# Border of the last stage of a two-layer gated transformer: two norms and three copies on VectorE, another order, three banks each for maxima and scores

## Chip, cores and metric

One core of a Trainium2 chip runs the kernel. The metric is the device time in microseconds of one execution, inputs and outputs in HBM. Engines: PE (TensorE matmul), VectorE (DVE in the rows), ACT (ScalarE), POOL (GpSimd), SP (SyncE, which here only issues DMAs).

## The reference

Sixteen batches of 256 tokens of width 256, all float32, through four gated residual steps. Only the last two matter here.

```python
x = x + jnp.tanh(g_xattn[0]) * _L0_xattn_ref(_layernorm(x, axis=-1), ctx_1024, ctx_1024)   # decayed running sum
x = x + jnp.tanh(g_ffn[0]) * _L0_ffn_ref(_layernorm(x, axis=-1), w_gate, w_up, w_down)     # fp4-quantised
x = x + jnp.tanh(g_xattn[1]) * _L1_xattn_ref(_layernorm(x, axis=-1), ctx_1024, ctx_1024, 16)
x = x + jnp.tanh(g_ffn[1]) * _L1_ffn_ref(_layernorm(x, axis=-1), w_fc, b_fc, w_proj, b_proj)
```

The third is attention with 16 heads of width 16, rotary embedding, a bias by position and a softmax. The fourth is `gelu(q(x) @ q(w_fc).T + b_fc)`, quantised again by `q`, times `q(w_proj).T`. `q` rounds blocks of 32 values to 3 bits behind the exponent of the block's largest magnitude.

## The kernel before, in words

The program is written engine by engine; the order on each engine is the order in its function, and semaphores (`wait_ge`, `then_inc`) tie them. `over_batches` calls a body once for each batch. A `Batch` has `shifted(n)`, the batch n further on or None past either end. `first`, `last` and `lead[0]` to `lead[5]` are batches 0, 15 and 0 to 5.

All of x stays in SBUF (`xres`). The first layer runs until about 337 us, attention from there to about 662, and the last stage, the second feed-forward, to the end. The eight PSUM banks of attention are two each: `a_ps_t` (for turned inputs), `a_ps_m` (products for the row maxima), `a_ps_s` (scores), `a_ps_pv` (values).

**Attention** (`at_body`). While batch b is exponentiated, b+1 is turned and its row maxima are taken, and b+2 is prepared. PE turns queries and keys in eight steps (`at_turn`, L586) that ACT copies out (`at_turned`, L953). Then come 16 groups m0 to m15 of products for the maxima (`at_scores_for_max`, L606), each of which VectorE reduces (`at_row_max`, L1558), with scores s2 to s15 between them (`at_scores`, L627; s0 and s1 stand in the turning). ACT exponentiates each score group (`at_exponent`, L962). After every two, PE multiplies with the values (`at_times_v`, L642, groups 0 to 7, quads of two), and ACT copies a quad out (`at_pv_out`, L968). PE turns this back (`at_turn_out`, L650) and VectorE adds it to `xres` (`at_add_attention`, L1565 to L1572), called the residual here. Even and odd groups use different halves of the array's rows.

Before the change m0 to m3, m6, m7, m10, m11, m14 and m15 lie in the two `a_ps_m` banks and the others in the two `a_ps_t` banks, so that from m6 on a group waits for the maximum four groups back; m2 and m3 wait for the one two back, m4 and m5 for none. A score waits for the exponential two back.

**The border.** The last attention batch has no next batch to turn. Into its place come: w3 and w4, the weights of the last stage, which GpSimd has rounded to codes and which PE turns (`turn_w34`) and ACT copies out (`w34_out`, L832); and the inputs of the leading batches. An input is made in these steps: statistics on VectorE (`ff_input_stats`), the power -1/2 on GpSimd (`ff_input_rstd`, L1228), the shift on VectorE (`ff_input_shift`), the norm on ACT (`ff_norm`, L1011), on VectorE the block's power of two, called its magic (`ff_input_magic`, L1622 to L1629), on GpSimd the sum with it (`ff_input_up`, L1234), on VectorE the codes (`ff_input_codes`, L1635), on PE the turning (`ff_turn_input`, L703) and on ACT the copy (`ff_input_out`, L1018).

**The last stage** (`ff_body`). PE makes four groups of 512 hidden values (`ff_fc`, L716 and L718), ACT the gelus (`ff_gelu`, L1024), VectorE their magic (`ff_hidden_magic`, L1643 to L1650), GpSimd the sum (`ff_hidden_up`, L1241), VectorE the codes (`ff_hidden_codes`, L1659), PE turns them (`ff_turn_hidden`) and multiplies with w4 (`ff_proj`, L743), and VectorE adds the residual (`ff_add_ffn`). In the body of batch b VectorE does hidden magic b+1, statistics b+6, codes b+3, hidden codes b and input magic b+4. `ff_hidden_magic(lead[0])` stands ahead of the loop.

The order of VectorE at the border before, from L1743 on:

```python
ff_input_stats(lead[0]); ff_input_stats(lead[1]); ff_input_shift(lead[0]); ff_input_shift(lead[1])
ff_input_magic(lead[0]); ff_input_stats(lead[2]); ff_input_shift(lead[2]); ff_input_codes(lead[0])
ff_input_magic(lead[1]); ff_input_stats(lead[3]); ff_input_codes(lead[1]); ff_input_shift(lead[3])
at_add_attention(last)
ff_input_magic(lead[2]); ff_input_stats(lead[4]); ff_input_codes(lead[2]); ff_input_shift(lead[4])
ff_input_magic(lead[3]); ff_input_stats(lead[5]); ff_hidden_magic(lead[0])
```

## Time and profile before

| | us |
|---|---|
| median of 3 runs | 815.8 (814.9 to 817.67) |
| the profiled execution | 816.15 |
| its span, first to last instruction | 814.0 |
| PE busy (matmul) | 701.7, 86% |
| VectorE busy | 691.9, 85% |
| ACT busy | 486.2, 60% |
| GpSimd busy | 431.4, 53% |
| mean granted clock of TensorE | 0.941 of 2.4 GHz |

Times in the rows are counted from the first instruction. Busy time of PE includes the tail of each pipelined matmul. What stands in brackets at the end of a timeline row is the idle time of the engine before it and what ended it. Neighbouring instructions of one line are merged, and "x2" tells how many. The largest groups of instructions are the exponentials (256 of 602 ns on ACT), the maxima (256 of 686 ns on VectorE) and the scores (512 matmuls on PE).

### The profile page before, as it was taken

How to read it: one execution, taken by the hardware profiler on the slowest of the kernel's cores; microseconds unless marked ns; L12 is line 12 of the kernel's file. 1: busy time of each engine (PE TensorE's matmuls, PEld its weight loads, DVE VectorE, ACT ScalarE, POOL GpSimd, SP SyncE). 2: the span in 40 equal slices, each digit the busy share in tenths (PEclk: the TensorE clock that was granted, in tenths of full speed). 3: DMA queues.
4: the chain of work that ended last, by engine and by line, in shares of the span. 5: the costliest groups of instructions: out<-in, count | busy, mean ns of one | idle time of the engine just before them, and what ended most of it. 6: DMA issues, size and time to landing. Idle time of an engine off the chain costs nothing.

```text
span 814.0 us, 16554 instructions
## 1 busy us (share of the span) xinstructions
PE 701.7 (86%) x5075; PEld 516.7 (63%) x5090; DVE 691.9 (85%) x1230; ACT 486.2 (60%) x955; POOL 431.4 (53%) x331
## 2 busy tenths in 40 slices
PE   1476999999999998789999999999999876877685
PEld 1365888888888876556666666666666433544454
DVE  5996888888888878779999999989898649999995
ACT  3354555455454443348887787888788674566653
POOL 3634664656656555644445555554444526665553
PEclk9588999999999999889999999999999687999998
DMA  8800000000000000010000000000001000100011
GB/s 271 252 33 0 2 1 1 0 0 0 0 0 1 1 2 0 1 53 2 3 3 1 1 1 2 1 1 1 1 1 53 2 1 0 40 26 26 27 39 52
DMA packets 17719, 18.35 MB, mean 23 GB/s; under 512 B 1670, under 2 KB 16912, under 8 KB 17680
## 3 DMA queue, kind: packets, MB, share of 16 engines
q1 hardware_dynamic: 17084, 17.66, 6.6%
q8 instruction: 21, 0.34, 0.2%
q10 hardware_dynamic: 596, 0.20, 0.1%
q14 instruction: 18, 0.15, 0.1%
HBM read 13.39 MB, written 4.19 MB: 22 GB/s over the span
## 4 chain that ended last, share of the span: by engine, by line
PE 56%; DVE 22%; issue 9%; ACT 6%; POOL 3%; DMA 1%; DVEq 1%; POOLq 0%; ACTq 0%
PE ps_o L547 9%; PE a_ps_t L586 7%; PE a_ps_pv L642 7%; PE a_ps_s L627 5%; PE a_ps_m L606 5%; DVE f_ps_small L1643 4%; PE ps_gu L511 4%; PE ps_gu L513 4%; PE ps_gu L512 4%; DVE f_hcode L1659 4%; PE a_ps_t L606 3%; DVE maxima L1558 2%; PE a_ps_pv L650 2%; ACT stack_t L953 1%; ACT probs L962 1%
## 5 line engine op out<-in xcount | busy, mean ns | idle before, releaser
L962 ACT ACTIVATE probs<-a_ps_s 128x512 f32<-128x512 f32 x256 | 147.8, 602 | 29.9 <-PE a_ps_s L627 25.4
L1558 DVE TENSOR_REDUCE maxima<-a_ps_m 128x2 f32<-128x512 f32 x160 | 103.0, 686 | 11.5 <-PE a_ps_m L606 11.3
L627 PE MATMUL a_ps_s<-stack_t 64*128 64x256 f32 x512 | 101.9, 314 | 3.4 <-ACT probs L962 1.8
L1192 POOL TENSOR_TENSOR stack<-roped,stack 128x512 f32<-128x512 f32 x32 | 42.7, 1335 | 109.7 <-DVE stack L1548 108.3
L547 PE MATMUL ps_o<-w2t,hqt 128*128 128x256 f32 (+1 forms) x384 | 99.1, 392 | 1.3 <-ACT hqt L880 0.7
L511 PE MATMUL ps_gu<-w1h,yth 128*128 128x352 f32 x256 | 87.5, 342 | 9.1 <-DVE h L1364 5.9
L953 ACT CAST stack_t<-a_ps_t 128x512 fp32r<-128x512 f32 x128 | 71.8, 585 | 31.5 <-PE a_ps_t L586 31.5
L642 PE MATMUL a_ps_pv<-probs,v_aug 128*32 128x256 f32 x1024 | 84.9, 404 | 2.9 <-ACT probs L962 2.9
L586 PE MATMUL a_ps_t<-idf,stack 128*128 128x128 f32 x512 | 77.2, 292 | 8.8 <-POOL stack L1192 5.1
L512 PE MATMUL ps_gu<-w1l,yth 128*128 128x352 f32 x256 | 84.1, 328 | 0.0
L513 PE MATMUL ps_gu<-w1h,ytl 128*128 128x352 f32 x256 | 83.8, 327 | 0.0
L547 PEld LDWEIGHTS ps_o<-w2t,hqt 128*128 128x128 f32 (+1 forms) x384 | 66.3, 189 | 22.1 <-issue 12.4
L627 PEld LDWEIGHTS a_ps_s<-stack_t 64*128 64x128 f32 x512 | 67.7, 190 | 16.7 <-ACT probs L962 9.4
L586 PEld LDWEIGHTS a_ps_t<-idf,stack 128*128 128x128 f32 x512 | 58.3, 147 | 25.4 <-ACT stack_t L953 8.4
L1558 DVE TENSOR_REDUCE maxima<-a_ps_t 128x2 f32<-128x512 f32 x96 | 63.1, 686 | 10.9 <-PE a_ps_t L606 10.9
L1159 POOL TENSOR_TENSOR hq<-hcode,hscale 128x1408 f32<-128x1408 bf16 x16 | 41.5, 2591 | 56.5 <-DVE hcode L1383 56.5
L606 PE MATMUL a_ps_m<-stack_t 64*128 64x256 f32 x320 | 66.3, 323 | 3.7 <-DVE maxima L1558 2.7
L872 ACT ACTIVATE sg<-ps_gu 128x352 f32<-128x352 f32 x64 | 29.7, 464 | 66.3 <-PE ps_gu L513 66.3
L606 PEld LDWEIGHTS a_ps_m<-stack_t 64*128 64x128 f32 x320 | 43.3, 188 | 34.3 <-DVE maxima L1558 18.8
L1241 POOL TENSOR_TENSOR f_hup<-f_h,f_hmag 128x2048 f32<-128x2048 f32 x16 | 58.2, 3640 | 9.1 <-DVE f_hcode L1659 8.1
L1024 ACT ACTIVATE f_h<-f_ps_fc 128x512 f32<-128x512 f32 x64 | 34.9, 596 | 42.0 <-POOL f_hup L1241 39.2
L511 PEld LDWEIGHTS ps_gu<-w1h,yth 128*128 128x128 f32 x256 | 49.4, 193 | 12.3 <-DVE h L1364 7.3
(181 smaller groups left out, 1680.9 us busy)
## 6 DMA issues: line engine op xcount, KB each, us to landing
xres<-in_x SPq DMA_DIRECT2D x16, 256.0 KB, 3.2
ctx<-in_ctx SPq DMA_DIRECT2D x16, 256.0 KB, 3.8
out_x<-f_y SPq DMA_DIRECT2D x16, 256.0 KB, 2.1
w1a_raw<-in_w_gate_up SPq DMA_DIRECT2D x1, 1024.0 KB, 7.3
w_raw<-in_w_fc SPq DMA_DIRECT2D x1, 1024.0 KB, 5.7
w_raw<-in_w_proj SPq DMA_DIRECT2D x1, 1024.0 KB, 4.8
w_raw<-in_w_down SPq DMA_DIRECT2D x1, 704.0 KB, 9.7
stack_t<-neg_max_t SPq DMA_DIRECT2D x32, 8.0 KB
```

What stands on the lines that cost most here:

```text
L511: nc.tensor.matmul(into, yth[:, kc, c, :], w1h[:, kc, cols], start=kc == 0, stop=False)
L512: nc.tensor.matmul(into, yth[:, kc, c, :], w1l[:, kc, cols], start=False, stop=False)
L513: ins = nc.tensor.matmul(into, ytl[:, kc, c, :], w1h[:, kc, cols], start=False, stop=kc == KD - 1)
L547: ins = nc.tensor.matmul(ps_o[:, c, :], hqt[0:rows, g, n, :], w2t[0:rows, k, :], start=k == 0, stop=k == KH0 - 1)
L586: ins = nc.tensor.transpose(a_ps_t[:, g % 2, (n * C + c) * P:(n * C + c + 1) * P], a_stack[:, b.par, which, c, 2 * pair:2 * pair + 2, :].r ...
L606: ins = nc.tensor.matmul(max_bank(m)[:, n, :], a_stack_t[b.par][rows, 0, pair, c * P:(c + 1) * P], a_stack_t[b.par][rows, 1, pair, :], sta ...
L627: ins = nc.tensor.matmul(a_ps_s[:, half, n, :], a_stack_t[b.par][rows, 1, pair, kc * P:(kc + 1) * P], a_stack_t[b.par][rows, 0, pair, :], ...
L642: ins = nc.tensor.matmul(a_ps_pv[32 * n:32 * n + 32, quad % 2, 0:T], a_v_aug[:, b.par, kc, 4 * quad + n, :], a_probs[:, (2 * g + n % 2) % ...
L953: nc.scalar.copy(a_stack_t[b.par][:, g % 2, pair:pair + 2, :].rearrange("p a t -> p (a t)"), a_ps_t[:, g % 2, :]).then_inc(a_t, 1)
L962: nc.scalar.activation(a_probs[:, u % 8], a_ps_s[:, u % 2], ACT.Exp).then_inc(a_exp, 1)
L1241: nc.gpsimd.tensor_tensor(f_blocks(f_hup[:, :]), f_blocks(f_h[:, b.par]), f_spread(f_hmag[:, b.par], F_NBH), ALU.add).then_inc(f_g_hup, 1)
L1558: nc.vector.tensor_reduce(a_maxima[:, b.par, c, 4 * quad + half:4 * quad + half + 3:2], max_bank(m), X, ALU.max).then_inc(a_v_max, 1)
```

## The change

- Three banks each: m_k lies in `a_ps_t[0]` if k mod 3 is 1, in `a_ps_m[0]` if it is 2, else in `a_ps_m[1]`. From s4 on a score lies in `a_ps_t[1]` or one of the `a_ps_s` banks by the same rule, in every batch but the last.
- `w34_out` is split: ACT copies w3 (`w3_out`), VectorE copies w4 (`w4_out`), earlier, since PE turns w4 after m=4 and no longer after m=8. PE turns the first input after m=10, not m=12.
- The norms of leading batches 2 and 3 go from ACT to VectorE, also named `ff_norm`.
- The copy of the last quad of values goes from ACT to VectorE (`at_last_pv_out`).
- VectorE's residual of the last batch goes behind the inputs of batches 2 and 3 and the statistics of 4 and 5; GpSimd's steps are reordered.

```diff
         def max_bank(m):
-            pair, half = m // 2, m % 2
-            if pair >= 2 and pair % 2 == 0:
-                return a_ps_t[:, half, :].rearrange("p (a t) -> p a t", t=T)
-            return a_ps_m[:, half]
+            if m % 3 == 1:
+                return a_ps_t[:, 0, :].rearrange("p (a t) -> p a t", t=T)
+            return a_ps_m[:, 0 if m % 3 == 2 else 1]
+        def score_bank(b, u):
+            if u < 4 or not b.shifted(1):
+                return a_ps_s[:, u % 2]
+            if u % 3 == 1:
+                return a_ps_t[:, 1, :].rearrange("p (a t) -> p a t", t=T)
+            return a_ps_s[:, 0 if u % 3 == 2 else 1]
+        def last_in_score_bank(b, u):
+            if not b.shifted(1):
+                return u - 2
+            return {2: 0, 3: 1, 5: 2, 6: 3}.get(u, u - 3)
+        M_LAST_IN_T, U_LAST_IN_T = MU - 3, SU - 3
...
 # at_turn
-                elif b.shifted(-1):
-                    pe.wait_ge(a_v_max, b.shifted(-1).count(MU, 2 * LAST_IN_TURN_BANKS + g + 1))
+                elif b.shifted(-1) and g == 0:
+                    pe.wait_ge(a_v_max, b.shifted(-1).count(MU, M_LAST_IN_T + 1))
+                elif b.shifted(-2):
+                    pe.wait_ge(a_exp, b.shifted(-2).count(SU, U_LAST_IN_T + 1))
 # at_scores_for_max
-                if m == 0 and b.shifted(-1):
+                if m >= 3:
+                    pe.wait_ge(a_v_max, b.count(MU, m - 2))
+                elif m == 1:
+                    pe.wait_ge(a_t, b.count(TG, TG - 1))
+                elif m == 2 and b.shifted(-1):
                     pe.wait_ge(a_mt, b.shifted(-1).count(1, 1))
-                if m in (4, 5):
-                    pe.wait_ge(a_t, b.count(TG, TG + m - 5))
-                elif m >= 2:
-                    pe.wait_ge(a_v_max, b.count(MU, group_in_same_max_bank(m) + 1))
                 elif b.shifted(-1):
-                    pe.wait_ge(a_v_max, b.shifted(-1).count(MU, MU + m - 1))
+                    pe.wait_ge(a_v_max, b.shifted(-1).count(MU, MU))
 # at_scores
-                if u >= 2:
-                    pe.wait_ge(a_exp, b.count(SU, u - 1))
+                if u == 4 and b.shifted(1):
+                    pe.wait_ge(a_t, b.shifted(1).count(TG, TG))
+                elif u >= 2:
+                    pe.wait_ge(a_exp, b.count(SU, last_in_score_bank(b, u) + 1))
 # at_body of PE
-                    if not nxt and m == 8:
+                    if not nxt and m == 4:
                         turn_w34(2)
                         turn_w34(3)
-                    if not nxt and m == 12:
+                    if not nxt and m == 10:
                         ff_turn_input(lead[0])
                 if not nxt:
-                    pe.wait_ge(a_w34, 4)
+                    pe.wait_ge(v_w4, 2)
 # at_body of ACT
-                    if not nxt and u == 9:
-                        w34_out(2)
-                        w34_out(3)
-                    if not nxt and u in (3, 7, 11):
+                    if not nxt and u in (3, 7):
                         ff_norm(lead[u // 4])
-                    if not nxt and u == 14:
+                    if not nxt and u == 12:
                         ff_input_out(lead[0])
-                at_pv_out(b, 3)
+                if nxt:
+                    at_pv_out(b, 3)
 # ACT, ahead of the last stage's loop
             ff_input_out(lead[1])
-            ff_norm(lead[3])
 # GpSimd, ahead of the last stage's loop
-            for b in lead[:3]:
-                ff_input_rstd(b)
+            ff_input_rstd(lead[0])
+            ff_input_rstd(lead[1])
             ff_input_up(lead[0])
+            ff_input_rstd(lead[2])
+            ff_input_up(lead[1])
             ff_input_rstd(lead[3])
-            ff_input_up(lead[1])
+            ff_input_up(lead[2])
             ff_input_rstd(lead[4])
-            ff_input_up(lead[2])
             ff_input_rstd(lead[5])
 # VectorE
+            def w4_out(at):
+                dve.wait_ge(t_w34, at + 3)
+                nc.vector.tensor_copy(w_proj_t[:, 4 * at:4 * at + 4, :].rearrange("p k n -> p (k n)"),
+                                      a_ps_m[:, at].rearrange("p a t -> p (a t)").bitcast(BF16)).then_inc(v_w4, 1)
+            def at_last_pv_out(b):
+                dve.wait_ge(a_t_pv, b.count(PG, PG))
+                dve.wait_ge(a_t_out, b.shifted(-1).count(2, 2))
+                nc.vector.tensor_copy(a_pv_t[:, 3, :], a_ps_pv[:, 1, 0:T]).then_inc(a_pv, 1)
+            def ff_norm(b):
+                dve.wait_ge(f_v_shift, b.count(1, 1))
+                dve.wait_ge(f_g_up, b.shifted(-2).count(1, 1))
+                for c in range(C):
+                    nc.vector.tensor_scalar(f_xn[:, b.par, c * D:(c + 1) * D], tiles(xres, b)[:, c, :], f_rstd[:, b.par, c:c + 1],
+                                            f_shift[:, b.par, c:c + 1], ALU.mult, ALU.add).then_inc(f_a_norm, 1)
...
             ff_input_magic(lead[0])
+            w4_out(0)
+            w4_out(1)
             ff_input_stats(lead[2])
             ff_input_shift(lead[2])
             ff_input_codes(lead[0])
             ff_input_magic(lead[1])
+            ff_norm(lead[2])
             ff_input_stats(lead[3])
             ff_input_codes(lead[1])
+            ff_input_magic(lead[2])
             ff_input_shift(lead[3])
-            at_add_attention(last)
-            ff_input_magic(lead[2])
+            ff_norm(lead[3])
             ff_input_stats(lead[4])
             ff_input_codes(lead[2])
+            ff_input_magic(lead[3])
             ff_input_shift(lead[4])
-            ff_input_magic(lead[3])
+            at_last_pv_out(last)
             ff_input_stats(lead[5])
+            at_add_attention(last)
             ff_hidden_magic(lead[0])
```

## Rows read from the trace of the kernel before

**Rows 1.** Windows: us, busy us (instructions) of each engine, granted clock, DMA share, GB/s.
```profile
...
374.00:621.00 247.00, 239.25 (x2265) 160.62 (x2262) 225.09 (x438) 198.72 (x402) 120.89 (x90) 1.00 0.01 3
645.65:654.25 8.60, 8.34 (x64) 4.44 (x62) 4.85 (x18) 7.40 (x15) 3.44 (x4) 0.60 0.00 0
663.34:670.71 7.37, 4.14 (x18) 1.74 (x20) 4.88 (x20) 5.98 (x12) 1.72 (x2) 0.93 0.00 1
...
661.00:666.00 5.00, 3.75 (x24) 2.06 (x23) 3.93 (x13) 4.94 (x9) 0.02 (x1) 1.00 0.00 0
672.00:814.00 142.00, 100.97 (x746) 65.48 (x757) 125.29 (x206) 78.24 (x123) 81.73 (x39) 0.90 0.09 30
```

**Rows 2.** Waits from 356 to 616: who for whom, total us, times, longest.
```profile
...
DVE maxima L1558 <- PE a_ps_t L606: 7.2, 14, 0.6
```

**Rows 3.** Timeline of VectorE, one batch: start, us, operation [idle before].
```profile
...
604.11 2.58 DVE L1558 TENSOR_REDUCE maxima<-a_ps_m 128x2 f32<-128x512 f32 x4 [0.47 <-PE a_ps_m L606]
607.23 1.29 DVE L1558 TENSOR_REDUCE maxima<-a_ps_t 128x2 f32<-128x512 f32 x2 [0.54 <-PE a_ps_t L606]
...
610.83 0.69 DVE L1548 CAST stack<-roped 128x1024 fp32r<-128x1024 f32 x1
...
614.42 1.29 DVE L1558 TENSOR_REDUCE maxima<-a_ps_m 128x2 f32<-128x512 f32 x2
```

**Rows 4.** Timeline of PE, the same batch.
```profile
...
604.17 0.64 PE L642 MATMUL a_ps_pv<-probs,v_aug 128*32 128x256 f32 x8
604.86 0.50 PE L606 MATMUL a_ps_m<-stack_t 64*128 64x256 f32 x2
...
606.12 0.64 PE L642 MATMUL a_ps_pv<-probs,v_aug 128*32 128x256 f32 x8
606.69 0.51 PE L606 MATMUL a_ps_t<-stack_t 64*128 64x256 f32 x4
...
612.30 0.64 PE L642 MATMUL a_ps_pv<-probs,v_aug 128*32 128x256 f32 x8
...
614.86 0.64 PE L642 MATMUL a_ps_pv<-probs,v_aug 128*32 128x256 f32 x8 [0.24 <-ACT probs L962]
```

**Rows 5.** Timeline of ACT, the same batch.
```profile
...
613.45 0.60 ACT L962 ACTIVATE probs<-a_ps_s 128x512 f32<-128x512 f32 x1 [0.42 <-PE a_ps_s L627]
...
614.20 0.61 ACT L962 ACTIVATE probs<-a_ps_s 128x512 f32<-128x512 f32 x1
```

**Rows 6.** Timeline of VectorE, the border.
```profile
...
661.33 0.26 DVE L1565 RECIPROCAL denom<-a_ps_pv 128x16 f32<-128x16 f32 x1 [7.08 <-PE a_ps_pv L650]
...
670.71 2.28 DVE L1643 TENSOR_REDUCE f_ps_small<-f_h 128x64 f32<-128x2048 f32 x1
...
673.55 2.29 DVE L1643 TENSOR_REDUCE f_ps_small<-f_h 128x64 f32<-128x2048 f32 x1
```

**Rows 7.** Timeline of PE, the border.
```profile
...
649.09 1.89 PE L463 MATMUL a_ps_m<-idb,w_codes 128*128 128x128 bf16 x16
...
660.64 1.09 PE L650 MATMUL a_ps_pv<-idf,pv_t 128*128 128x128 f32 x8 [0.49 <-ACT pv_t L968]
...
662.86 0.39 PE L703 MATMUL f_ps_h<-idb,f_xcode 128*128 128x128 bf16 x4
664.50 0.39 PE L716 MATMUL f_ps_fc<-bias,ones 128*128 128x512 bf16 x1 [1.25 <-ACT f_xt L1018]
```

**Rows 8.** Timeline of ACT, the border.
```profile
...
656.62 0.63 ACT L962 ACTIVATE probs<-a_ps_s 128x512 f32<-128x512 f32 x1
...
661.90 2.06 ACT L1024 ACTIVATE f_h<-f_ps_fc 128x512 f32<-128x512 f32 x4
...
665.35 2.54 ACT L1024 ACTIVATE f_h<-f_ps_fc 128x512 f32<-128x512 f32 x4
```

**Rows 9.** Two lines of VectorE: count, ns min/median/max, first and last start.
```profile
...
L1527 DVE TENSOR_SCALAR qn<-xres,a_mv,a_rstd x26: 400/822/1252, 378.2 to 601.3; 128x256 f32 x24, 128x256 f32<-128x256 f32 x2
...
L1659 DVE TENSOR_TENSOR f_hcode<-f_hup,f_hmag x32: 1211/1218/1227, 678.1 to 805.2; 128x1024 bf16<-128x1024 f32 x32
```

More of the change, by code:

```diff
@@ L626, in at_scores @@
                     pair = 2 * quad + n
-                    ins = nc.tensor.matmul(a_ps_s[:, half, n, :], a_stack_t[b.par][rows, 1, pair, kc * P:(kc + 1) * P],
+                    ins = nc.tensor.matmul(score_bank(b, u)[:, n, :], a_stack_t[b.par][rows, 1, pair, kc * P:(kc + 1) * P],
                                            a_stack_t[b.par][rows, 0, pair, :], start=True, stop=True)
@@ L961, in at_exponent @@
                     act.wait_ge(a_t_pv, b.shifted(-1).count(PG, (u + 8) // 2 + 1))
-                nc.scalar.activation(a_probs[:, u % 8], a_ps_s[:, u % 2], ACT.Exp).then_inc(a_exp, 1)
+                nc.scalar.activation(a_probs[:, u % 8], score_bank(b, u), ACT.Exp).then_inc(a_exp, 1)
             def at_pv_out(b, quad):
```

20 lines of the change are left out of this document (8 added, 12 removed).

## The prediction

> **What bounds the kernel now.** I read the windows by stage first, then the waits and the timelines of one attention batch and of the border. In the attention loop PE is busy 239 of 247 us and VectorE 225, at the full granted clock of 2.4 GHz (1.00); in the last stage VectorE is busy 125 of 142 us and PE 101 [rows 1]. So the loop is a close race of two engines, and the last stage is VectorE's: what moves VectorE's start there moves the end.
>
> The loop takes sixteen batches, 18.4 and 18.6 us in turn. Each has a stretch of turning and one of sixteen max groups m0 to m15, between which PE does scores s2 to s15 and seven value groups. VectorE reduces a group every 0.60 us and has one hole: after m3 it is idle 0.54 us until m4 arrives [rows 3]. The waits show it in 14 batches of 14, 7.2 us in all [rows 2]. Its reason stands on PE: m2 and m3 wait for the maxima of m0 and m1 (one bank apart), each breaks PE's stream, the second value group starts only at 606.12 and m4 at 606.69 [rows 4]. The stretch is closed by another chain: s14 and s15, their exponentials at 613.45 and 614.20 with a copy of values between, and the last value group at 614.86, after which the next turn starts at 615.43 [rows 4, 5].
>
> At the border VectorE waits from 654.25 to 661.33 for the last attention's turned output: the residual stands ahead of the inputs of batches 2 to 4. It takes all these up behind it and reaches the first hidden magic at 670.71, though the gelus it needs had ended at 663.96; the second starts at 673.55 [rows 6, 8]. From there on VectorE hardly rests.
>
> **The change, part one: three banks each.** m_k now waits for the maximum of m_(k-3), and the scores rotate through three banks. I walk the batch from 603.49 with the durations of [rows 3 to 5], a wait's latency 0.05. m2 has nothing to wait for and starts when value group 0 ends (604.17 + 0.57 = 604.74 against 604.86); m3 waits only for m0's maximum (604.81) and goes beside it. Value group 1 then starts at 605.53 (606.12 before) and m4 at 606.10 (606.69): 0.59 earlier. The data are there at 606.60, VectorE comes free at 606.55, so its hole shrinks from 0.54 to about 0.05. From then VectorE is fed without a break and is 0.59 early.
> PE meets new waits, because the max groups had four banks in the second half and have three: value group 3 ends at 609.0, m9 waits for m6's maximum until 609.18 (0.19); m10 for m7's until 609.79 (0.25); m12 for m9's. m9's maximum follows the cast at 610.83 by 0.60 and ends now at 610.83 + 0.60 + 0.69 - 0.59 = 611.53, so m12 and s13 start at 611.6 after 0.44 idle, and value group 5 at 612.02 instead of 612.30. Behind it s14 is ready 0.31 earlier, the exponentials move from 613.45 to 613.14 and the last value group from 614.86 to 614.55. So of the 0.59 gained in front, 0.31 reach the next turn. The turn of a batch waits for m13's maximum and an exponential of the batch before; both are over 1 us old. The last max group's reduction ends 0.1 us after that turn starts, as the turning of the maxima comes 0.9 us later it hides.
> The loop has 14 such batches besides the one with w4's magic, in which VectorE is the bound and a hole of 0.5 us is traded for a PE block one group earlier (0), and the first one, where PE runs at the lower clock and the turn waits one maximum longer (0.0, bounds -0.3 and +0.4). Sum: 14 x -0.31 = -4.3 us. Bounds: -0.59 x 14 = -8.3 (all of it arrives) and 0.
>
> **Part two: the border, ahead of the residual.** VectorE's new list: magic 0 (ends 645.73 as before), two w4 copies, everything it had between, two norms; then the copy of the last values, stats 5, the residual, hidden magic 0.
> *w4 copies.* PE turns w4 right after s6, by the order of its instructions at about 645.5 (an estimate: four score groups, 0.43 us each at the low clock, and a value group less than now) instead of 649.09; the 16 transposes take 1.9 us at this stretch's clock of 0.60 [rows 1, 7]. The second bank is there at 647.4. VectorE's copy of 1024 columns isn't in the trace; nearest are 1.22 us (1024 elements of codes, two inputs) [rows 9] and 0.69 (the cast of 1024) [rows 3]. I take 1.1, so 648.5; with the ends 648.1 to 648.7. PE's and ACT's work doesn't grow: ACT loses two copies of 1.0 and a norm, which shortens its way to its last exponential by some 1.3 us (656.6 to 657.2 before [rows 8]).
> *Norms.* The same form on 128x256 takes 0.40 us in its shortest case, 0.82 as median, 1.25 at most [rows 9]. The long ones overlap GpSimd's elementwise work. Here each norm starts in the moment in which a magic also releases GpSimd's up step, so I take about 1.5 for each pair, 3.0 for both; bounds 1.5 and 5.0. The Trainium skill's page "SBUF — State Buffer" (section "SBUF: two separate sides") says that a VectorE operation in a two-port mode and a GpSimd operation hold one shared port pair exclusively, whichever starts first; by it both pairs of norms lose one up step each, by a free port the forecast would be 1.5 us lower. The 1.25 against 0.40 agrees with the lock.
> *The list's length.* The work from 645.65 to the wait was 4.85 us busy and that behind the residual up to the first hidden magic 4.88 [rows 1]; less 1.2 for stats 5, which stay behind, 8.5 us. With norms 3.0 and one exposed wait for GpSimd's power step of batch 2 (0.85: its start used to be covered, now nothing of VectorE stands between): 648.5 + 8.5 + 3.0 + 0.85 = 660.9. Call it D. The last value group is out by 659, so VectorE is later than PE there: the 7.08 us of idle is filled and the last values' copy starts at D.
> *Behind D.* What is queued on PE behind that copy: the turned output, which waits for it, the last two groups of batch 0's first product (2.22 us from 660.64 to 662.86 [rows 7]), then batch 1's. With 0.45 for the copy the gelus of batch 0 end at D + 3.4 = 664.3; before near 664.0. ACT's table load, which stood between the last value copy and the first of these gelus, now goes under the wait. Batch 1's four products and gelus took 664.50 to 667.89, 3.4 us [rows 7, 8]; with ACT's input copy ahead they end at D + 7.2 = 668.1. VectorE: copy 0.4, stats 5 1.2, residual 2.0 (661.33 to 663.34 before, where the window begins [rows 1, 6]), first hidden magic at D + 3.8 = 664.7 instead of 670.71, over at 667.5; the second starts at 668.2 instead of 673.55. After it stand the same steps as before, with GpSimd's hidden up released 6 us earlier, and VectorE full. **Gain 5.3 us**, bounds below.
>
> **Sum.** The profiled execution is 816.15 us (span 814.0), 0.35 above the median of 815.8. 816.15 - 4.3 - 5.3 = **806.6 us**.
>
> **Rivals.**
> *The border at the lower clock.* PE's clock is 1.00 from 661 to 666 but 0.60 from 645 to 654 [rows 1]. The change leaves PE with some 2 us of nothing before D. If the products behind it then run at 1.2 GHz, they take twice as long: 1.7 more to the gelus of batch 0, 2.5 more for batch 1, so the second hidden magic comes at 672.4, and the border gives 1.1 only: 816.15 - 4.3 - 1.1 = 810.7. For it: the idle is new. Against: PE was idle there before, and had the full clock right after. "TensorE: Matmul & The Clock Gate" of the Trainium skill (section "HAM oscillation — how this bites in real kernels") says that a gap in PE's work sends it to half rate, and the next burst pays; by it this rival is the case.
> *The loop gives nothing.* The new waits ahead of m9, m10 and m12 sum to 0.9 us of PE and eat the 0.59: 816.15 - 5.3 = 810.9. For: PE has only 8 us of idle in 247.
> *The loop gives the whole hole:* 816.15 - 8.3 - 5.3 = 802.6. For: VectorE and PE are both early; against: the chain over the exponentials closes the stretch.
> *Slower: the three-bank ring.* PE takes its instructions in order; a max group that waits holds the scores and the value group behind it, and these feed ACT. If the front isn't won (m4 still late, because s4 now waits for the last turned copy, or m3 doesn't run beside m2), the 0.9 us of waits stay with some 0.5 exposed in each batch: 14 x 0.5 = +7.0, and 816.15 + 7.0 - 5.3 = 817.9 (822 with the lower clock). It decides from +0.38 us a batch, where it eats the border's 5.3.
> *The change doesn't do what it says:* VectorE's list is much longer (norms at 5.0, copies at 1.22, more waits for GpSimd), D beyond 666: 816 with an idle loop.
>
> **How the numbers follow.** Forecast 0.45, lower clock 0.15, loop nothing 0.17, whole hole 0.12, no gain at all 0.05, slower 0.06. The range 802.5 to 813.0 holds the first four and the mixtures of the second and third. A run can be told from no change beyond 0.3%, here 2.4 us: faster 0.86, same 0.07, slower 0.07.
>
> **What would show it.** Right: batches of 18.1 and 18.3 us; the idle of VectorE ahead of m4 below 0.1 (now 0.54); waits of PE for maxima ahead of the second half's groups; the last value group 0.3 nearer to the start of the stretch. At the border VectorE idle under 2 us between 641 and 665 of before's time, the second hidden magic 27.2 us behind the end of the last residual but one, at 641.0 (32.5 now). Wrong: a period above 18.5, a granted clock under 0.8 over batch 1's products, norms over 1.25 each, or a VectorE that reaches the value copy before PE's last value group ends.

## The result, and the profile after

The changed kernel takes 810.02 us (median of 6 runs, 809.08 to 810.57) against 815.74 (6 runs, 813.4 to 817.86) for the kernel before: ratio 0.9919, 95% interval 0.9905 to 0.9934. Faster, as forecast, and inside the range; but 3.4 us above the 806.6 forecast. The profiled execution took 810.57, its span is 808.5 (814.0 before).

A period is the time from one turning of the maxima on PE to the next; sixteen batches make fifteen of them. Stage by stage, the 5.5 us of span are: up to the first reduction of maxima +1.1 (340.08 to 341.17; code that the change doesn't touch), 14 periods of the loop (the first and 13 ordinary ones) -3.28, the last period 0.0 (20.15 and 20.14), from the last turning of the maxima to the second hidden magic -2.11, from there to the last hidden magic 0.0 (121.50 and 121.54), and the rest -1.30 (19.00 to 17.70). Two of the six terms are the change's: 5.4 us, where 9.6 were forecast.

Windows of the changed kernel (us, busy us (instructions) of PE, PEld, VectorE, ACT, POOL, granted clock, DMA share, GB/s), which answer to [rows 1]:
```profile
374.00:618.80 244.80, 231.62 (x2277) 148.86 (x2278) 224.84 (x439) 200.71 (x403) 121.61 (x91) 1.00 0.01 3
...
656.00:661.00 5.00, 0.77 (x10) 0.29 (x4) 4.77 (x15) 1.05 (x2) 1.92 (x2) 0.93 0.01 2
661.00:663.50 2.50, 2.50 (x11) 1.85 (x11) 1.80 (x8) 0.00 (x0) 1.57 (x2) 0.50 0.00 0
663.50:666.00 2.50, 1.56 (x11) 0.66 (x9) 1.60 (x3) 1.67 (x3) 0.14 (x1) 0.95 0.00 0
```
The first row is the loop. Between 661 and 663.5 PE works without a pause at clock 0.50, 1.2 GHz. Before, 661 to 666 had 1.00 [rows 1].

**The loop.** VectorE (start, us, operation [idle before <- what ended it]) in the batch that answers to [rows 3]. Lines are shifted by the edit: maxima L1579, maximum products L619, values L657.
```profile
602.21 0.69 DVE L1579 TENSOR_REDUCE maxima<-a_ps_m 128x2 f32<-128x512 f32 x1 [0.82 <-PE a_ps_t L619]
602.82 0.68 DVE L1579 TENSOR_REDUCE maxima<-a_ps_t 128x2 f32<-128x512 f32 x1
603.42 1.28 DVE L1579 TENSOR_REDUCE maxima<-a_ps_m 128x2 f32<-128x512 f32 x2
604.73 0.69 DVE L1579 TENSOR_REDUCE maxima<-a_ps_t 128x2 f32<-128x512 f32 x1
```
The hole before m4 is gone: from 602.21 to the end of the stretch there is no idle entry. But the idle ahead of the first maximum is 0.82 instead of 0.47 [rows 3]. What VectorE won in the middle it spends waiting for the next batch, since another chain sets that. The waits tell the same: the row of [rows 2] is now this one, and it means another place. A reader who only looks at the total would think that the wait ahead of m4 grew from 7.2 us.
```profile
DVE maxima L1579 <- PE a_ps_t L619: 11.4, 14, 0.9
```
PE in that batch, for [rows 4]:
```profile
601.59 0.38 PE L619 MATMUL a_ps_m<-stack_t 64*128 64x256 f32 x1
...
604.19 0.38 PE L619 MATMUL a_ps_t<-stack_t 64*128 64x256 f32 x1
...
609.67 0.38 PE L619 MATMUL a_ps_m<-stack_t 64*128 64x256 f32 x1 [0.29 <-DVE maxima L1579]
...
610.11 0.64 PE L657 MATMUL a_ps_pv<-probs,v_aug 128*32 128x256 f32 x8
...
612.67 0.64 PE L657 MATMUL a_ps_pv<-probs,v_aug 128*32 128x256 f32 x8 [0.26 <-ACT probs L975]
```
m4 starts 2.60 us behind m0, before 3.20 (603.49 to 606.69); value group 5 at 8.52, forecast 8.53; the last value group at 11.08, before 11.37: 0.3 earlier, as walked.

**The border.** VectorE, for [rows 6]:
```profile
646.15 1.47 DVE L1512 COPY w_proj_t<-a_ps_m 128x1024 bf16<-128x1024 bf16 x2 [1.72 <-PE a_ps_m L474]
...
649.63 0.16 DVE L1636 SCALAR_TENSOR_TENSOR f_shift<-f_ps_small,f_rstd 128x2 f32<-128x2 f32 x1 [0.82 <-POOL f_rstd L1238]
...
651.33 1.46 DVE L1643 TENSOR_SCALAR f_xn<-xres,f_rstd,f_shift 128x256 f32<-128x256 f32 x2
...
660.23 0.42 DVE L1518 COPY pv_t<-a_ps_pv 128x256 f32<-128x256 f32 x1
...
665.23 2.29 DVE L1671 TENSOR_REDUCE f_ps_small<-f_h 128x64 f32<-128x2048 f32 x1 [0.87 <-ACT f_h L1035]
...
669.24 2.29 DVE L1671 TENSOR_REDUCE f_ps_small<-f_h 128x64 f32<-128x2048 f32 x1 [1.12 <-ACT f_h L1035]
```
The 7.08 us of idle are filled, the two waits at the end are new: VectorE stands before both hidden magics until their gelus end. PE, for [rows 7]:
```profile
639.21 0.51 PE L642 MATMUL a_ps_s<-stack_t 64*128 64x256 f32 x4 [2.10 <-DMA stack_t<-neg_max_t]
...
655.85 0.64 PE L657 MATMUL a_ps_pv<-probs,v_aug 128*32 128x256 f32 x8
660.71 1.97 PE L665 MATMUL a_ps_pv<-idf,pv_t 128*128 128x128 f32 x8 [4.23 <-DVE pv_t L1518]
...
662.90 1.02 PE L733 MATMUL f_ps_fc<-w_fc_t,f_xt 128*128 128x512 bf16 x2
...
663.97 0.59 PE L733 MATMUL f_ps_fc<-w_fc_t,f_xt 128*128 128x512 bf16 x2
```
PE waits 4.23 us for the value copy, then the turned output takes 1.97 us (1.09 before) and a pair of products 1.02, a moment later 0.59. And ACT, for [rows 8]: the load of the gelu's table indeed lies ahead of the wait, but two of batch 0's gelus wait 6.91 us for the products queued behind the turned output.
```profile
654.67 1.28 ACT L1035 ACT_TABLE_LOAD   x1
655.96 1.08 ACT L1035 ACTIVATE f_h<-f_ps_fc 128x512 f32<-128x512 f32 x2
663.96 1.25 ACT L1035 ACTIVATE f_h<-f_ps_fc 128x512 f32<-128x512 f32 x2 [6.91 <-PE f_ps_fc L733]
```

### The profile page after: what moved, and what is told of

Read it like the earlier page. It is cut to its first block, busy times and chain, and to the rows that moved or that the text cites. A ratio compares the mean times of both kernels' runs of the same rounds, so it can differ in the third digit from the quotient of the medians.

```text
span 808.5 us, 16554 instructions
## 1 busy us (share of the span) xinstructions
PE 691.2 (85%) x5075; PEld 503.9 (62%) x5090; DVE 694.7 (86%) x1237; ACT 483.2 (60%) x948; POOL 432.8 (54%) x331
## 4 chain that ended last, share of the span: by engine, by line
PE 50%; DVE 26%; issue 11%; ACT 5%; DMA 3%; POOL 2%; DVEq 1%; SPq 1%; POOLq 0%; ACTq 0%
PE ps_o L558 9%; PE a_ps_t L599 7%; DVE maxima L1579 5%; PE a_ps_pv L657 5%; PE ps_gu L522 4%; PE ps_gu L524 4%; PE ps_gu L523 4%; DVE f_hcode L1687 4%; DVE f_ps_small L1671 4%; PE a_ps_s L642 3%; PE a_ps_m L619 3%; DMA ctx<-in_ctx 2%; PE a_ps_t L619 2%; PE a_ps_pv L665 2%; ACT stack_t L966 1%
## 5 line engine op out<-in xcount | busy, mean ns | idle before, releaser
L1579 DVE TENSOR_REDUCE maxima<-a_ps_m 128x2 f32<-128x512 f32 x176 | 116.1, 681 | 16.8 <-PE a_ps_t L619 11.3
L975 ACT ACTIVATE probs<-a_ps_s 128x512 f32<-128x512 f32 x196 | 115.7, 601 | 24.3 <-PE a_ps_s L642 19.6
L619 PE MATMUL a_ps_m<-stack_t 64*128 64x256 f32 x352 | 80.9, 327 | 10.2 <-DVE maxima L1579 8.8
L657 PE MATMUL a_ps_pv<-probs,v_aug 128*32 128x256 f32 x1024 | 83.6, 399 | 3.5 <-ACT probs L975 3.5
L642 PE MATMUL a_ps_s<-stack_t 64*128 64x256 f32 x392 | 79.3, 312 | 4.5 <-DMA stack_t<-neg_max_t 2.1
L619 PEld LDWEIGHTS a_ps_m<-stack_t 64*128 64x128 f32 x352 | 50.1, 187 | 50.9 <-issue 29.3
L642 PEld LDWEIGHTS a_ps_s<-stack_t 64*128 64x128 f32 x392 | 53.7, 189 | 14.7 <-issue 6.6
L1579 DVE TENSOR_REDUCE maxima<-a_ps_t 128x2 f32<-128x512 f32 x80 | 54.5, 681 | 3.2 <-PE a_ps_t L619 2.6
```

Source lines behind the costliest of these rows:

```text
L619: ins = nc.tensor.matmul(max_bank(m)[:, n, :], a_stack_t[b.par][rows, 0, pair, c * P:(c + 1) * P], a_stack_t[b.par][rows, 1, pair, :], sta ...
L642: ins = nc.tensor.matmul(score_bank(b, u)[:, n, :], a_stack_t[b.par][rows, 1, pair, kc * P:(kc + 1) * P], a_stack_t[b.par][rows, 0, pair, ...
L657: ins = nc.tensor.matmul(a_ps_pv[32 * n:32 * n + 32, quad % 2, 0:T], a_v_aug[:, b.par, kc, 4 * quad + n, :], a_probs[:, (2 * g + n % 2) % ...
L975: nc.scalar.activation(a_probs[:, u % 8], score_bank(b, u), ACT.Exp).then_inc(a_exp, 1)
L1579: nc.vector.tensor_reduce(a_maxima[:, b.par, c, 4 * quad + half:4 * quad + half + 3:2], max_bank(m), X, ALU.max).then_inc(a_v_max, 1)
```

## The experiments

The columns are read from the timelines of each kernel's profiled execution. "Loop" is the time over 14 periods, from the first turning of the maxima to the last but one. The next five columns count from the last turning of the maxima (636.51 before, 634.31 in the changed kernel): first score of the last batch, which waits for the DMA of its row maxima; last value copy; first and second hidden magic; and the second less what the first score lies beyond 3.47, which differs by up to 1.4 between runs with the same code there. "Ratio" is to the kernel before on the same chip.

| kernel | ratio, interval | loop | score | value copy | magic 0 | magic 1 | less score |
|---|---|---|---|---|---|---|---|
| before | 1 | 260.01 | 3.47 | 23.70 | 34.19 | 37.04 | 37.04 |
| changed | 0.9919, 0.9905 to 0.9934 | 256.73 | 4.90 | 25.92 | 30.92 | 34.93 | 33.50 |
| after_again (changed) | 0.9914, 0.9896 to 0.9932 | 256.59 | 4.03 | 25.14 | 30.36 | 34.36 | 33.80 |
| banks_only | 0.9968, 0.9952 to 0.9984 | 256.76 | 3.71 | 23.45 | 33.94 | 36.79 | 36.55 |
| border_only | 0.9959, 0.9944 to 0.9973 | 261.11 | 3.47 | 24.55 | 29.42 | 33.42 | 33.42 |
| max3_score2 | 0.9969, 0.9956 to 0.9982 | 261.34 | 4.17 | 25.85 | 29.72 | 33.39 | 32.69 |
| max2_score3 | 1.0169, 1.014 to 1.0197 | 274.02 | 3.47 | 24.54 | 29.76 | 33.76 | 33.76 |
| residual_first | 0.9947, 0.9929 to 0.9966 | 256.64 | 4.43 | 21.93 | 32.00 | 34.85 | 33.89 |
| warm_pe | 0.992, 0.9891 to 0.995 | 256.67 | 3.47 | 25.13 | 31.99 | 35.99 | 35.99 |
| products_ahead | 0.9901, 0.9877 to 0.9926 | 256.64 | 3.48 | 24.55 | 29.13 | 31.98 | 31.97 |
| magic_ahead | 0.9912, 0.9896 to 0.9928 | 256.67 | 3.47 | 24.56 | 26.09 | 33.16 | 33.16 |
| norms_on_act | 0.9903, 0.9886 to 0.9919 | 256.79 | 3.69 | 24.03 | 30.55 | 33.40 | 33.18 |
| w4_on_act | 0.9883, 0.9866 to 0.99 | 256.67 | 4.10 | 24.69 | 29.78 | 32.62 | 31.99 |
| ahead_and_norms | 0.9895, 0.988 to 0.991 | 256.67 | 4.23 | 25.91 | 27.95 | 35.03 | 34.28 |

The landing moves the value copy with it: with the same amount taken off, the copy starts 24.49 behind the turning in the changed kernel, 24.58 in after_again and 24.55 in border_only.

Stages that no kernel here edits also differ: the first reduction starts between 338.7 and 341.9, the tail behind the last hidden magic is 17.7 or 18.7 to 19.4, and from the second hidden magic to the last it takes 121.0 to 121.6, but 122.29 in max2_score3 and 123.17 in banks_only. So the ratios tell parts of 2 us and more, and the columns tell smaller ones. But the columns stand for one execution, and not always a typical one: that of residual_first is the fastest of 12 (808.09, median 811.9), those of w4_on_act and ahead_and_norms are the slowest of 5 (810.25 and 810.36, medians 808.16 and 808.35).

**banks_only** and **border_only**: one part each. The first keeps before's orders, norms and copies and has the three-bank rings, the second the reverse. The changed kernel ran beside them as **after_again**, unedited.
```diff
 # border_only, on the changed kernel
-            if m % 3 == 1:
-                return a_ps_t[:, 0, :].rearrange("p (a t) -> p a t", t=T)
-            return a_ps_m[:, 0 if m % 3 == 2 else 1]
+            pair, half = m // 2, m % 2
+            if pair >= 2 and pair % 2 == 0:
+                return a_ps_t[:, half, :].rearrange("p (a t) -> p a t", t=T)
+            return a_ps_m[:, half]
...
```


> The kernel before with nothing but the new banks and their waits. Theory A, the two parts of the change add up and the loop's is the larger: attention periods of 18.14 and 18.31 us (18.36 and 18.62 before), from first value group to first max group 11.08 and 11.16 us (11.38 and 11.47), and a time 3.4 us below the kernel before. Theory B, the loop's gain is only real together with a border that takes it up, because VectorE at the border waits for PE: the periods fall the same, but under 1.5 us of it reach the end. Forecast of the prediction for this part alone: -4.3 us.

> The changed kernel with the banks and waits of before in the attention loop. Theory A: periods 18.36 and 18.62 as before, and a time 2.1 to 3.6 us below the kernel before: 5.3 as forecast, less 1.8 for PE's low clock behind the last value copy, less up to 1.4 for a late landing of the last batch's row maxima. Theory B (the gains belong together): 4 us or more.

> The changed kernel once more, unchanged, for a second profile. In the first one PE began the last batch's scores 4.90 us after the turning of the maxima, 3.47 before the change; and the last value copy was followed by products at 1.2 GHz. Theory C, chance: 3.5 us this time, and a border (from the last turning of maxima to the second hidden magic) of 33.5 in place of 34.9 us. Theory D, a cost of the change (what PE, SyncE and ACT do there is not moved, so I doubt it): 4.9 again. The clock: low again behind the value copy, as PE is idle for over 4 us ahead of it whatever the phase.

Measured: 813.67, 812.74 and 809.23 us against 816.28. The rings alone give periods of 18.14 and 18.30 and a border of 36.8, the border alone 18.37 and 18.6 and a border of 33.4. By ratio the parts are -2.6 and -3.3 us, and the whole change is -7.0 beside them: they add, within the intervals, and both are real. The border's 3.6 us in the trace (37.04 to 33.42) are what the edit is worth when the DMA of the row maxima lands as it did before. In border_only's loop column two things hide that the edit doesn't touch: its first period is 20.84 (19.71 before), and its last, which the column leaves out, 19.23 (20.15 before), with the clock at 1.00 over its last 4 us where before it was 0.57. max3_score2's last period is short in the same way, 19.04.

after_again has PE's idle time and lower clock behind the value copy once more:
```profile
659.77 1.73 PE L665 MATMUL a_ps_pv<-idf,pv_t 128*128 128x128 f32 x8 [2.42 <-DVE pv_t L1518]
...
661.73 1.06 PE L733 MATMUL f_ps_fc<-w_fc_t,f_xt 128*128 128x512 bf16 x2
```
The idle is 2.42 us here, for 4.23 in the first trace, and the lower level is the same.

**max3_score2** and **max2_score3**: only one of the two rings has three banks.
```diff
 # max3_score2
-            if u < 4 or not b.shifted(1):
-                return a_ps_s[:, u % 2]
-            if u % 3 == 1:
-                return a_ps_t[:, 1, :].rearrange("p (a t) -> p a t", t=T)
-            return a_ps_s[:, 0 if u % 3 == 2 else 1]
+            return a_ps_s[:, u % 2]
...
 # max2_score3
-            if m % 3 == 1:
-                return a_ps_t[:, 0, :].rearrange("p (a t) -> p a t", t=T)
-            return a_ps_m[:, 0 if m % 3 == 2 else 1]
+            return a_ps_m[:, m % 2]
...
```


> The changed kernel with three banks for the maxima but the two of before for the scores, each score waiting for the exponential two back. Theory E, the maxima's ring gives nearly all: periods within 0.06 us of 18.14 and 18.31, time within 0.8 us of the changed kernel. Theory F, the third score bank is what lets PE run ahead to m4 (s6 and s7 no longer wait for the exponentials two back): periods 0.15 us or more longer, time 2 to 3.5 us above the changed kernel, and VectorE's hole ahead of m4 back to 0.3 us or more.

> The changed kernel with only the two a_ps_m banks for the maxima, each group waiting for the maximum two back, and three banks for the scores. The ring of three for the maxima alone (scores on two) had given nothing: periods 18.45 and 18.68. Theory F1, the scores' third bank alone makes the loop's gain: periods near 18.14 and 18.31. Theory F2, both are needed, since a maxima ring of two stops PE ahead of each group until VectorE is through, and VectorE then has a hole ahead of every group of a value pair: periods 18.6 or more, time 4 us or more above the changed kernel.

Measured: periods of 18.45 and 18.68 without the third score bank, a little longer than before's, and 19.44 and 19.58 without the third maximum bank. VectorE's waits, max3_score2:
```profile
DVE maxima L1571 <- PE a_ps_t L613: 11.4, 14, 0.9
DVE maxima L1571 <- PE a_ps_m L613: 8.8, 16, 2.9
```
and max2_score3:
```profile
DVE maxima L1575 <- PE a_ps_m L615: 26.4, 42, 2.9
```
In the changed kernel the wait for `a_ps_m` is 3.7 us in 2 times; in max3_score2 it comes 14 more times, once in a batch, and is 5.1 us more. That PE's scores wait for an exponential again and hold the maximum groups behind them is my reading of PE's order, and not shown by itself. The gain of 0.2 to 0.3 us a batch needs both rings; neither gives it alone, and each alone is a loss against the kernel before, whose maxima had four banks in the second half of a batch.

max3_score2 shows one thing more, at the border. Its last values come late, PE is idle only 0.55 us ahead of the turned output, and the order behind the value copy is that of the changed kernel:
```profile
661.71 1.09 PE L657 MATMUL a_ps_pv<-idf,pv_t 128*128 128x128 f32 x8 [0.55 <-DVE pv_t L1510]
...
662.85 0.59 PE L725 MATMUL f_ps_fc<-w_fc_t,f_xt 128*128 128x512 bf16 x2
```
At the full clock it is 7.54 us from the value copy to the second hidden magic, where the changed kernel took 9.01.

**residual_first**: the last value copy and the residual at the place where the kernel before had the residual; norms and w4 copies as in the changed kernel.
```diff
             ff_input_codes(lead[1])
+            at_last_pv_out(last)
+            at_add_attention(last)
             ff_input_magic(lead[2])
...
-            at_last_pv_out(last)
             ff_input_stats(lead[5])
-            at_add_attention(last)
             ff_hidden_magic(lead[0])
```


> The changed kernel with the last value copy and the last batch's residual ahead of the third input magic, near their old place; all else as changed. Theory G, the order is what fills VectorE's idle time: VectorE waits about 2 us for PE's last value group and 1.5 for the turned output, the first hidden magic comes about 33.3 us behind the last turning of maxima (30.4 and 30.9 changed), the second 36.1 (34.4 and 34.9), the time 1.3 to 2 us above the changed kernel. Theory H, the order hardly matters, since PE then has no long idle and keeps its clock, and batch 1's products come early: the second hidden magic within 0.5 us of the changed kernel's.

VectorE:
```profile
653.72 0.42 DVE L1518 COPY pv_t<-a_ps_pv 128x256 f32<-128x256 f32 x1 [2.05 <-PE a_ps_pv L657]
654.90 0.26 DVE L1586 RECIPROCAL denom<-a_ps_pv 128x16 f32<-128x16 f32 x1 [0.75 <-PE a_ps_pv L665]
...
663.79 2.28 DVE L1671 TENSOR_REDUCE f_ps_small<-f_h 128x64 f32<-128x2048 f32 x1
...
666.64 2.29 DVE L1671 TENSOR_REDUCE f_ps_small<-f_h 128x64 f32<-128x2048 f32 x1
```
VectorE idles 2.8 us before and in the residual, but the gelus are long done when it comes to the hidden magics, which stand back to back. The second comes at 33.89 (less score) against 33.50 and 33.80, within 0.5 us as the second theory said. So in this trace the order of which the change consists at this place is worth 0.1 to 0.4 us: it turns 2.8 us of idle ahead of the residual into 2.0 us ahead of the hidden magics. The other 3.2 us of the border (37.04 to 33.89) come with the other moves, the copies, the norms and the earlier turnings, taken together; no run parts them.

The medians don't settle it. By ratio residual_first is 2.3 to 2.7 us slower than the changed kernel, more than the first theory's 1.3 to 2, and the intervals hardly overlap. Its twelve executions spread from 808.09 to 814.99, and the trace is of the fastest. What the order is worth in a typical execution stays open.

**warm_pe**: 16 more matmuls on PE between the last value group and the turned output, whose result nobody reads.
```diff
+            for _ in range(16):
+                nc.tensor.matmul(f_ps_h0[:, :], idb[:, :], w_fc_t[:, 0, 0:512], start=True, stop=True)
             at_turn_out(last)
```


> The changed kernel with 16 matmuls whose results nobody reads (128x128 by 512 columns, into the bank of the first input's turned codes) between the last value group and the turned output, where PE is idle for 4.2 us. Theory I, PE's low clock behind the value copy costs the border 1.5 us: the turned output takes 0.9 us (1.97 changed), the gelus of batch 0 end 3.5 us after the value copy starts (5.0 and 5.2), the second hidden magic comes 1.5 us earlier, time 1.5 us lower. Theory J, the low clock is hidden by VectorE's own residual, or the clock falls whatever PE does: no change.

PE:
```profile
657.47 4.15 PE L813 MATMUL f_ps_h<-w_fc_t,idb 128*128 128x512 bf16 x16
661.46 1.04 PE L665 MATMUL a_ps_pv<-idf,pv_t 128*128 128x128 f32 x8
...
662.55 0.59 PE L733 MATMUL f_ps_fc<-w_fc_t,f_xt 128*128 128x512 bf16 x2
```
The filler was too long: the value copy came at 657.60, the turned output had to wait until 661.46, and magic 1 is 2.2 to 2.5 us later than in the changed kernel. Some 0.6 of that is not the filler's: the value copy itself waited 0.51 for PE's last values, which came at the lower clock. So neither theory held. But the price of the clock can be read: with PE at 1.00 the turned output is 1.04 instead of 1.97, and from its start to the last gelu of batch 0 it is 3.0 us instead of 4.5. The lower clock costs 1.5 us there.

**products_ahead**: the products that need no attention output go ahead of the turned output, so that PE has them to do while it would wait.
```diff
-            at_turn_out(last)
...
-            for u in range(4):
-                ff_fc(lead[1], u)
+            ff_fc(lead[1], 0)
+            ff_fc(lead[1], 1)
+            at_turn_out(last)
+            ff_fc(lead[1], 2)
+            ff_fc(lead[1], 3)
```


> The changed kernel with PE's second half of batch 0's products, batch 1's turned input and the first two of batch 1's products moved ahead of the turned output, into PE's idle 4.2 us. They need nothing from VectorE's value copy; in the order of the changed kernel they are queued behind it. Theory K, what is queued on PE behind the copy sets the second hidden magic: VectorE doesn't wait for gelus any more (0.87 and 1.12 us of idle ahead of the two magics), the first comes 30.0, the second 32.9 us behind the last turning of maxima (30.4 and 34.4 changed), time 1.5 to 2 us below the changed kernel. Theory L, the last stage is paced by GpSimd's hidden sum or ACT and gives it back within two batches: the second magic is early, the time the same.

VectorE:
```profile
658.67 0.42 DVE L1520 COPY pv_t<-a_ps_pv 128x256 f32<-128x256 f32 x1
...
661.25 0.26 DVE L1588 RECIPROCAL denom<-a_ps_pv 128x16 f32<-128x16 f32 x1 [0.96 <-PE a_ps_pv L665]
...
663.25 2.29 DVE L1673 TENSOR_REDUCE f_ps_small<-f_h 128x64 f32<-128x2048 f32 x1
...
666.10 2.29 DVE L1673 TENSOR_REDUCE f_ps_small<-f_h 128x64 f32<-128x2048 f32 x1
```
and PE:
```profile
659.30 0.39 PE L731 MATMUL f_ps_fc<-bias,ones 128*128 128x512 bf16 x1 [0.94 <-ACT f_xt L1031]
...
660.61 1.04 PE L665 MATMUL a_ps_pv<-idf,pv_t 128*128 128x128 f32 x8
```
Both waits before the hidden magics are gone, the clock is 1.00 from 659 to 665, and magic 1 comes at 31.97: 5.1 us ahead of before, where 5.3 were forecast. Its median of 806.79 us is the shortest here. That it beats the changed kernel is read from this column (1.5 to 1.8 us); the intervals of the ratios overlap.

Four more on top of products_ahead ask what is left.

**magic_ahead** has the first hidden magic ahead of the residual.
```diff
-            at_add_attention(last)
             ff_hidden_magic(lead[0])
+            at_add_attention(last)
```


> On top of products_ahead: VectorE does the first hidden magic ahead of the last residual. Theory (VectorE's queue sets the border): the 0.96 us that VectorE waits for the turned output and the wait in front of the residual are filled with hidden magic 0, which then starts about 26.2 us after the last turning of the maxima (29.1 in products_ahead) and the second at about 31.0 instead of 32.0: 1.0 us less, 805.8. Rival (the turned output or the gelus of batch 1 end last): the second hidden magic stays at 32.0 and so does the time, 806.8.

VectorE, and GpSimd (POOL) in the same stretch:
```profile
660.01 2.28 DVE L1673 TENSOR_REDUCE f_ps_small<-f_h 128x64 f32<-128x2048 f32 x1
...
663.02 0.76 DVE L1592 TENSOR_TENSOR attn<-a_ps_pv,denom 128x256 f32<-128x256 f32 x2
663.81 3.28 DVE L1595 SCALAR_TENSOR_TENSOR xres<-attn,gates,xres 128x512 f32<-128x512 f32 x1
...
667.08 2.28 DVE L1673 TENSOR_REDUCE f_ps_small<-f_h 128x64 f32<-128x2048 f32 x1
```
```profile
662.90 3.64 POOL L1253 TENSOR_TENSOR f_hup<-f_h,f_hmag 128x2048 f32<-128x2048 f32 x1 [1.02 <-DVE f_hmag L1680]
```
Both theories fail. Magic 0 comes at 26.09, as the first said (26.2), yet magic 1 is 1.2 us later. The step that adds the attention to x takes 3.28 us instead of 0.75, and ends 0.55 us after GpSimd's sum, which ends at 666.54: it stood still for as long as GpSimd worked. Its neighbours, which read PSUM, took 0.76 for two, where 0.69 is usual. The Trainium skill's page "SBUF — State Buffer" (section "SBUF: two separate sides") says that an operation of VectorE with two inputs in SBUF and one of GpSimd that reads SBUF can't run together, and that the second waits for the whole of the first. The trace agrees. In the order of the change the residual stands ahead of the hidden magic that releases this sum, and is safe from it: an effect of the order that I had not priced. It isn't safe from GpSimd's shorter sum for an input (1.05 us): in border_only that one ends at 663.29 and the residual's add, started at 662.49, at 663.84, 1.35 us long; in max3_score2 it is 1.34 and in max2_score3 1.01, and each ends 0.54 or 0.55 after the sum. In the changed kernel the add starts at 663.61, as that sum ends (663.64), and takes 0.75.

**norms_on_act** puts both norms back on ACT; **ahead_and_norms** does this and magic_ahead's edit.
```diff
 # ACT
-                    if not nxt and u in (3, 7):
+                    if not nxt and u in (3, 7, 11):
                         ff_norm(lead[u // 4])
...
+            ff_norm(lead[3])
 # VectorE
-            ff_norm(lead[2])
...
-            ff_norm(lead[3])
```


> On top of products_ahead: the norms of leading batches 2 and 3 back on ACT, the first after exponential 11, the second after the last exponential, ahead of the gelus. Theory (VectorE's list sets the copy of the last values, ACT has room): VectorE is 2.9 us shorter, the value copy starts near 22 us after the last turning of the maxima instead of 24.6, the second hidden magic at 29.5 instead of 32.0, and the time is 804.3. Rival (ACT is as full as VectorE there): 2.2 us of norms on ACT put off the last value group and the gelus, so that VectorE waits for values or gelus and the second hidden magic comes at 32 or later: 806.8 or more, and the move of the norms to VectorE was worth its 2.9 us.

> On top of products_ahead: the norms of batches 2 and 3 on ACT and hidden magic 0 ahead of the residual, both. Theory (VectorE's queue alone sets the border): the gains add, the second hidden magic starts 28.5 to 29 us after the last turning of the maxima instead of 32.0, and the time is 803.5 to 804. Rival (with VectorE's queue shortened, the gelus of batches 0 and 1 are the bound): hidden magic 0 itself waits for them, the second hidden magic stays at 30.5 to 32, and the time is 805.3 to 806.8.

norms_on_act, VectorE and ACT:
```profile
661.79 0.26 DVE L1589 RECIPROCAL denom<-a_ps_pv 128x16 f32<-128x16 f32 x1 [2.91 <-PE a_ps_pv L665]
```
```profile
654.81 1.12 ACT L1024 ACTIVATE f_xn<-xres,f_shift,f_rstd 128x256 f32<-128x256 f32 x2
655.95 1.28 ACT L1037 ACT_TABLE_LOAD   x1
657.25 2.06 ACT L1037 ACTIVATE f_h<-f_ps_fc 128x512 f32<-128x512 f32 x4
```
VectorE comes to the value copy only 0.7 us earlier (two waits for norms, 0.30 and 0.66, stand in its list) and then idles 2.91: the norm of batch 3 on ACT pushes table load, gelus and the copy of batch 1's input back (the last gelu of batch 1 by 1.2), PE's turned output is queued behind the products that need it, and magic 1 is 1.2 us later. The rival held, though the move of the norms to VectorE is worth 1.2 us here and not the 2.9 that it named. In ahead_and_norms, VectorE:
```profile
666.25 3.28 DVE L1596 SCALAR_TENSOR_TENSOR xres<-attn,gates,xres 128x512 f32<-128x512 f32 x1
```
In its trace the losses add: magic 1 at 34.28, later than in the changed kernel. Its ratio doesn't show it, being no higher than that of either edit alone.

**w4_on_act** puts the w4 copies back on ACT, the turning of w4 staying early.
```diff
 # ACT, between exponentials
+                    if not nxt and u == 6:
+                        w4_out(0)
+                        w4_out(1)
 # VectorE
-            w4_out(0)
-            w4_out(1)
```


> On top of products_ahead: both w4 copies back on ACT, between exponentials 6 and 7, with w4 still turned after m4. Theory (moving the copies to VectorE was not worth anything by itself): VectorE saves 1.5 us of copies and the 1.7 us in which it waited for the turning of w4, ACT's 2.0 us are hidden, and the second hidden magic comes 1 to 3 us earlier, 804 to 806. Rival (ACT is the bound in that stretch): exponentials 7 to 15 and the last value group come 2 us later, VectorE waits for them, and the time is 806.8 to 808.

ACT and VectorE:
```profile
646.06 1.93 ACT L847 COPY w_proj_t<-a_ps_m 128x1024 bf16<-128x1024 bf16 x2
```
```profile
649.58 0.69 DVE L1660 TENSOR_REDUCE f_ps_small<-f_xn 128x16 f32<-128x512 f32 x1 [2.46 <-ACT f_xn L1032]
```
Neither theory: magic 1 at 31.99 stands where it stood. VectorE saves copies and wait, and then waits 2.46 us for the norm of batch 1, which ACT does behind the copies. Its median is 808.16, its ratio the lowest of all, with an interval that overlaps that of products_ahead. In its trace only the value copy comes earlier (24.06 for 24.55, the landing taken off), which reaches neither magic; but the trace is of its slowest execution. Whether it is better stays open.

## Why the prediction was right, and where it was too large

The direction, the two mechanisms and the range were right; the sum was too large in both parts. That 810.57 lies on the 810.7 of the rival "the border at the lower clock" is chance: that rival has -4.3 and -1.1 us for the two parts, and they were -3.3 and -2.1.

**Periods.** Forecast 18.1 and 18.3; measured 18.14 and 18.31. m4 0.60 earlier (0.59 forecast), value group 5 at 8.52 (8.53), the last value group 0.30 (0.31). For the batch that it walked, the walk was right to a few hundredths, and "0.31 of 0.59 reach the next turn" too.

**Their sum.** 14 x -0.31 was the wrong size: -3.28 measured. Three things make the 1.1 us. There are 13 such periods and not 14 (0.3): the 14 waits of [rows 2] count the first period too, whose wait is 0.2 us and not 0.5. In seven of the 13, 0.07 to 0.11 come back: from the turning of the maxima to m0 it was 5.49 us (598.00 to 603.49) and is 5.56 (596.03 to 601.59), as the first score comes later behind that turning, and the period is 0.22 shorter and not 0.31 (18.36 to 18.14). That is 0.6 us over the loop. That the score waits there for the DMA of the row maxima is my reading. And the first period, forecast at 0.0, is 19.87 instead of 19.71. The last was 0.0, as said.

**w4 copies.** Two took 1.47, forecast 2.2; they ended 13.3 us behind the last turning of the maxima, which is 11.9 without the DMA's 1.43, forecast 12.0 (648.5).

**Norms.** 1.46 and 1.47 for a pair, forecast 1.5: in each pair one took 0.40 and the other, beside GpSimd's sum, 1.14 or 1.15. The wait for the power step was 0.82, forecast 0.85.

**D** (the start of the last value copy). Forecast 24.4 behind the last turning of the maxima, measured 25.92, of which 1.43 are the DMA of the row maxima (4.90 instead of 3.47); border_only and products_ahead, without that, have 24.55. The step was right.

**Behind D.** This step failed. It said "the gelus of batch 0 end at D + 3.4", the first hidden magic starts at D + 3.8, the second at D + 7.3 (668.2). Measured: 4.98, 5.00 and 9.01. I had left the full clock as the likely case since PE kept it over an idle time before; there it had 0.49 us of idle ahead of the turned output [rows 7], here 4.23, and the products behind it ran at 1.2 GHz. border_only had 2.43 us of idle and after_again 2.42, and their products ran at the lower level just so (a pair in 1.06, and D to magic 1 in 8.87 and 9.22). All 14 traces fall in two groups: behind 2.42 to 4.23 us of idle (changed, after_again, border_only, max2_score3) the pair of products behind the turned output took 1.02 to 1.06, and behind 0.55 or less, in the other ten, 0.59. My own rival "the border at the lower clock" came in by 1.6 to 1.9 us of the 4.2 it was priced at: the clock was back at 0.95 when batch 1's products came, and these were to pay 2.5. I had counted "2 us of nothing before D" as small. By the rule of the Trainium skill's page "TensorE: Matmul & The Clock Gate" (section "HAM oscillation — how this bites in real kernels") that I quoted against the forecast, a gap is paid by the next burst. The trace agrees, and the rival should have had more than 0.15.

So, in the profiled run: loop -3.3 for -4.3; border -2.1 for -5.3, of which +1.4 is the DMA, +1.7 the turned output and the first products at the lower clock with what waits for them, and 0.1 lies in D; first layer +1.1 and tail -1.3, which no step spoke of and which cancel. max3_score2 confirms the reading: same order, full clock, D to magic 1 in 7.54, forecast 7.3. products_ahead has 7.43, with PE kept busy and fewer products queued behind the copy.

**The other rivals.** "The loop gives nothing" and "slower: the three-bank ring" are out by the periods. The second shows in max2_score3 and max3_score2, where one ring is missing: with two banks for the maxima a period is 1.0 to 1.1 us longer than before, so the third bank is what keeps that loss away. "The whole hole" is out: 0.35 us of it reappears ahead of the first maximum. "The change doesn't do what it says" is out by D.

**Open.** Why the DMA of the last row maxima lands between 3.47 and 4.90 us behind their turning, in kernels with the same code up to it, and whether the changed kernel draws late landings oftener (4.90 and 4.03 in its two traces). It is issued 0.8 us behind that turning in both, and no run here isolates it. The same holds for the tail of 17.7 or some 19 us: in all six traces with the short tail the clock is full from 8 to 4.5 us before the end, and in the eight others it is 0.53 to 0.68 there. Open too is what each move at the border is worth by itself, and what residual_first's order costs in a typical execution.

## What to carry to other kernels

When an engine's wait is filled by moving its work ahead, write down who waited with it: here VectorE's 7 us of idle became 4 us of PE's, just ahead of PE's most urgent work, and a third of the gain forecast there (1.7 of 5.3 us) was lost to a lower clock. Give the newly idle engine something useful from behind the wait (products_ahead) before looking for more. And a hole in one engine of a close race is worth what the closing chain of the period lets through, which a walk over the rows gave to 0.01 us for one batch here; what comes back behind it (0.07 in every second batch) has to be walked too, and the periods have to be counted. Last, one trace is one execution: before a few tenths are read from it, see where it stands among the others.

## What the runs showed of the hardware

- An add of VectorE with two SBUF inputs, 0.75 us by itself, took 3.28 beside a GpSimd operation of 3.64 us (magic_ahead, ahead_and_norms) and 1.35 beside one of 1.05 (border_only), and ended 0.55 after it each time. Two operations that read PSUM took 0.76 instead of 0.69 beside it (magic_ahead), and a reduction with one SBUF input kept its 2.29 (norms_on_act, 666.64, beside a sum from 666.68).
- A copy of 128x1024 bf16 out of PSUM takes 0.69 us on VectorE (changed) and 1.01 on ACT (before, w4_on_act).
- With 4.23 us of idle ahead of the turned output (changed) and with 2.43 (border_only), a pair of products behind it took 1.02 and 1.06, the lower level; with 0.55 (residual_first, max3_score2) 0.59, the full one.
- The gelu's table load (1.28 us) begins at 654.67 in the changed kernel, while PE is still making the product that this gelu reads (654.67 to 655.26): it isn't held by the gelu's wait.
